# Staging the next sample's normalised input: low parts and transfers on POOL in four rows, two of them in the sum buffer

## The chip, the cores and the metric

One core of a Trainium2 chip. The metric is the device time of one execution in microseconds; the median of three runs counts. Engines are named as in the profile: PE is TensorE, ACT ScalarE, DVE VectorE, POOL GpSimd, and SP issues most transfers.

## The reference

The input is x with 8 samples of 512 channels and 32 x 32 positions (N = 1024). Two layers follow each other.

```python
# layer 0: attention without softmax, then batch norm over samples and positions
K, Q, V = conv1x1(X, Wq, bq), conv1x1(X, Wk, bk), conv1x1(X, Wv, bv)     # 8 heads of 64
M = einsum('bhmn,bhen->bhme', K, V)
Out = conv1x1(einsum('bhme,bhmn->bhen', M, Q), Wo, bo) + X
y = batch_norm(Out) * gamma + beta
# layer 1: group norm, 8-head softmax attention over 1024 positions, projection, residual
xn = group_norm(y, 32 groups) * gamma + beta
q, k, v = split(w_qkv @ xn + b_qkv)
a = softmax(q.T k / sqrt(64)) v
out = y + w_proj @ a + b_proj
```

## The kernel before

All large products are made from split operands. A float32 matrix is held as a high part (what ACT writes as fp32r) and a low part (the matrix less its high part), and a product is three matmuls: high x high, high x low and low x high.

Layer 0 runs over the 8 samples and ends at about 680 us of the span. It stores its result, not yet normalised, to DRAM (`y_dram`); its statistics give a scale and a bias per channel and sample for layer 1's group norm (`xn_scale`, `xn_bias`). The change touches layer 1 alone.

Layer 1 goes sample by sample, b = 0 to 7, and each sample in four pairs of heads (`PAIRS`). A pair has four tiles for the queries and keys, 16 tiles that only find the row maxima, and for each of 8 blocks of keys scores, exponentials (ACT, L685, into `probs`, a ring of three slots of 2 heads x 1024), weighing (PE, L1336, into `psum[2]`) and the running sum of the probabilities (POOL, L506, into `p_sum`). The tiles of the next pair are made among the scores of this one. A sample ends with 8 value tiles for the next sample (`v_tile`), among them the matmuls that add `p_sum` over the keys (`sums`, L1350), then 8 projection tiles, whose results are added to the residual on DVE (L1089). The residual is loaded into slots 0 and 1 of `probs` (`res32`), scaled by ACT (L713) and stored from there. Then come the next sample's pair 0 and its query and key tiles for pair 1 (L1285).

The normalised input of a sample must lie in SBUF as high and low parts (`xn`, 2 x 4 x 1024 per partition). There is room for one sample only, so that of sample b + 2 is *staged* while sample b ends: it is made from `y_dram` and stored to `xn_dram`, and SP loads it in one 4 MB transfer in the third pair of sample b + 1. Samples 1 to 7 are staged: sample 1 in the opening of layer 1, beside sample 0's value tiles and maxima, the other six at the ends of samples 0 to 5. The ends of samples 6 and 7 stage nothing.

Staging is done in 8 units of 512 columns (`UNITS`). For each, ACT waits for the unit's load into `y_half` (two halves in turn), normalises it in place (`norm_unit`, L602), writes its high part into slot 2 of `probs` (`stage_r`, L608), and DVE subtracts (`norm_lo`, L927) to write the low part beside it. ACT's queue then issues the store of both parts (`store_xn`, L593, 512 KB) and the load of the unit after the next (L596, 256 KB). SP loads the first two units of a sample (L388). Four units are made before ACT's `hid_hi` of the last pair, four after the residual is scaled. DVE's four early subtractions stand behind the copies of the first four value tiles (L966), the four late ones behind its adds of projection tiles 2 to 5.

Each engine works its own instructions in the order written, and semaphores order the engines among each other. `work_full` and `work_free` count PE's tiles and their evictions: tiles go through two banks, so PE starts tile n only when tile n - 2 is evicted. The six staging samples are one loop on SP, ACT and DVE (L435, L718, L1093); PE's loop holds samples 0 to 6 (L1447), POOL's too (L509).

ACT waits for all staging stores before the exponentials of a sample use slot 2 again.

Of the kernel before, what the change touches and what calls it, by code (L numbers as in the profile page):

```python
# [69 lines left out]
def build(nc, x, wq_t, wv_t, wk, wo_t, bq0, bv0, bk0, bo0, gamma0, beta0, gamma1, beta1, w1, bqkv1, bproj1, out):  # L70
# [14 lines left out]
    with ExitStack() as ctx:  # L85
# [42 lines left out]
        stage_r = probs[:, SLOTS - 1].rearrange("p h (a n) -> p h a n", a=2).bitcast(F32R)  # L128
        y_half = a1.take(2, HALF)
# [3 lines left out]
        recip = a1.take(NH, HALF)  # L133

# [75 lines left out]
        y_half_loaded = [sem("y_half_loaded0"), sem("y_half_loaded1")]  # L210
# [5 lines left out]
        xn_lo_done = sem("xn_lo_done")  # L216
        xn_stored = [sem("xn_stored0"), sem("xn_stored1")]
# [54 lines left out]
        UNITS = NH * CT  # L272
        EARLY = UNITS // 2

        def unit(u):
            return u // NH, slice(u % NH * HALF, (u % NH + 1) * HALF)
# [54 lines left out]
        def _(sp):  # L331
# [68 lines left out]
            load_y(1)  # L400
# [3 lines left out]
            def batch1(b, last, stage):  # L404
# [9 lines left out]
                if not last:  # L414

                    for half in xn_stored:
                        sp.wait_ge(half, (b + 1) * (UNITS // 2) * 16)
# [25 lines left out]
        def _(pool):  # L443
# [48 lines left out]


            def batch1(b, last):
                for p in range(PAIRS):
                    last_pair = last and p == PAIRS - 1
                    pairs = b * PAIRS + p
                    for i in range(1, NT):
                        for half in range(1 if last_pair else NH):
                            cols = slice(half * HALF, (half + 1) * HALF)  # L500
                            if i == 1 and half == 0:
# [5 lines left out]
                                               probs[:, i % SLOTS, :, cols], ALU.add).then_inc(sum_step, 1)  # L507

            with pool.Fori(0, B - 1) as b:  # L509
                batch1(b, False)  # L510
            batch1(B - 1, True)

        @block.scalar
        def _(act):
# [74 lines left out]
            def store_xn(tb, u):  # L589

                j, cols = unit(u)
                act.wait_ge(xn_lo_done, tb * UNITS + u + 1)
                act.dma_start(f(xn_dram[tb, :, :, j, cols]), f(stage_r[:, u % 2])).then_inc(xn_stored[u % 2], 16)  # L593
                if u + 2 < UNITS:
                    j, cols = unit(u + 2)
                    act.dma_start(y_half[:, u % 2], y_v[tb, :, j, cols]).then_inc(y_half_loaded[u % 2], 16)  # L596

            def norm_unit(tb, u, scale, bias):

                made = (tb - 1) * (UNITS // 2) + u // 2  # L600
                act.wait_ge(y_half_loaded[u % 2], (made + 1) * 16)
                act.activation(y_half[:, u % 2], y_half[:, u % 2], ACT.Identity, scale=scale(u // NH),  # L602
                               bias=bias(u // NH)).then_inc(xn_made, 1)
                act.wait_ge(xn_made, tb * UNITS + u + 1)
                if u >= 2:

                    act.wait_ge(xn_stored[u % 2], made * 16)
                act.activation(stage_r[:, u % 2, HI], y_half[:, u % 2], ACT.Copy).then_inc(xn_hi_done, 1)  # L608
                if u:
                    store_xn(tb, u - 1)  # L610
                if u == UNITS - 1:
                    store_xn(tb, u)
# [21 lines left out]
            for u in range(UNITS):  # L634
                norm_first(u)
            for i in range(QK):
                qk_hi(0, 0, i)
            for i in range(NT):
                act.wait_ge(v_first_full, i + 1)
                act.activation(v_t[:, i], bank(i % CT), ACT.Copy).then_inc(v_first_done, 1)  # L640
                norm_unit(1, i, lambda j: xn_scale[:, j, 1:2], lambda j: xn_bias[:, j, 1:2])

            def batch1(b, last, stage):
                work.start(b)
                for p in range(PAIRS):
# [10 lines left out]
                    for i in range(NT):  # L656
                        before = slot_row(i)
                        for half in range(NH):
                            cols = slice(half * HALF, (half + 1) * HALF)
                            act.wait_ge(scores_full, pairs * 2 * NT + 2 * i + half + 1)  # L660
                            if i < SLOTS and p == 0:
# [7 lines left out]
                                if i == SLOTS - 1 and half == 0:  # L669

                                    for stored in xn_stored:
                                        act.wait_ge(stored, (b if last else b + 1) * (UNITS // 2) * 16)
# [26 lines left out]
                def stage_units(us_):  # L699
                    for u in us_:  # L700
                        norm_unit(b + 2, u, lambda j: next_norm[:, 0, j:j + 1], lambda j: next_norm[:, 1, j:j + 1])

                if stage:
# [3 lines left out]
                    stage_units(range(EARLY))  # L707
# [7 lines left out]
                if stage:  # L715
                    stage_units(range(EARLY, UNITS))

# [6 lines left out]
        def _(dve):  # L724
# [200 lines left out]
            def norm_lo(tb, u):  # L925
                dve.wait_ge(xn_hi_done, tb * UNITS + u + 1)
                dve.tensor_tensor(stage_r[:, u % 2, LO], y_half[:, u % 2], f(stage_r[:, u % 2, HI]), ALU.subtract).then_inc(xn_lo_done, 1)  # L927

# [91 lines left out]
            for m in range(MAXES):  # L1020
                max_tile(m)
                if m % 2:
                    norm_lo(1, m // 2)
            max_join()

            def batch1(b, last, stage):
                work.start(b)
                for p in range(PAIRS):
# [20 lines left out]
                    if more:  # L1049
                        if p == 0:  # L1050
                            dve.wait_ge(max_ready, pairs + 1)
                        for m in range(MAXES):
# [3 lines left out]
                            if p == 1 and m == 4 and stage:  # L1056

                                dve.wait_ge(xn_hi_done, (b + 2) * UNITS)
# [25 lines left out]
                for t, (o, half) in enumerate(proj_tiles(last)):  # L1084
# [400 lines left out]
```

## Time and profile before

| | |
|---|---|
| median of 3 runs | 2802.01 us (2800.88 to 2802.41) |
| the profiled execution | 2800.88 us, span 2799.2 us |
| PE busy | 2644.6 us, 94% of the span |
| DVE / ACT / POOL busy | 1577.1 / 992.0 / 1122.4 us |
| mean granted clock of TensorE | 0.975 |
| `xn_dram` stores on ACT's queue | 56 of 512 KB, 3.4 us to landing |

The span runs from the first to the last instruction of the profiled execution. Busy time is the time in which an engine worked; what decides is when PE stands still, and what released it.

### The profile page before, as it was taken

What the parts mean: (1) busy time and instruction counts of PE and PEld (TensorE: products, weight loads), DVE (VectorE), ACT (ScalarE), POOL (GpSimd) and SP (SyncE); (2) the same over time, 40 slices, a digit from 0 to 9 for tenths busy, and PEclk for the clock granted to TensorE, in tenths of its full rate; (3) what the DMA queues carried; (4) which work ended last, traced back from release to release, by engine and by line L of the source; (5) the groups of instructions that cost most, each with busy time, mean ns of one, the idle gap of its engine ahead of it and who ended that gap; (6) DMA issues with size and microseconds to landing.
All of it is one profiled execution on the core that took longest, in us unless ns stands there. A gap on an engine that the chain in (4) does not pass through costs nothing.

```text
span 2799.2 us, 38416 instructions
## 1 busy us (share of the span) xinstructions
PE 2644.6 (94%) x13908; PEld 1740.0 (62%) x13908; DVE 1577.1 (56%) x1755; ACT 992.0 (35%) x1214; POOL 1122.4 (40%) x522
## 2 busy tenths in 40 slices
PE   8999999998899989998998999899989998999998
PEld 6888788886555565565556555655565565557554
DVE  5545455545566636754764566466636754764665
ACT  3232222332343433433442444343433433442433
POOL 3320000000076426534571576076426534671762
PEclk9999999998999999999999999999999999999999
DMA  5331111112301230232204110401230232202001
GB/s 184 127 118 35 40 45 60 60 60 91 120 24 76 80 125 23 91 104 86 83 31 161 51 76 34 171 23 76 79 125 23 91 105 85 91 16 105 16 16 61
DMA packets 75530, 214.53 MB, mean 77 GB/s; under 512 B 9712, under 2 KB 9712, under 8 KB 74480
## 3 DMA queue, kind: packets, MB, share of 16 engines
q1 hardware_dynamic: 50512, 159.41, 15.6%
q10 hardware_dynamic: 21280, 40.38, 4.3%
q0 software_dynamic: 3584, 12.58, 1.3%
q8 instruction: 109, 1.79, 0.3%
q14 instruction: 45, 0.37, 0.0%
HBM read 141.05 MB, written 71.30 MB: 76 GB/s over the span
## 4 chain that ended last, share of the span: by engine, by line
PE 76%; DVE 9%; DMA 5%; issue 3%; ACT 3%; POOL 3%; ACTq 1%; DVEq 0%; POOLq 0%
PE psum L1336 14%; PE psum L1285 13%; PE psum L1320 12%; PE psum L1103 12%; PE psum L1122 6%; PE psum L1295 6%; DMA a_all<-y_dram 5%; DVE small L944 4%; PE psum L1146 4%; PE psum L1174 3%; POOL a_all L506 2%; PE psum L1350 2%; PE psum L1217 2%; DVE a_all L974 1%; PE psum L1114 1%
## 5 line engine op out<-in xcount | busy, mean ns | idle before, releaser
L506 POOL TENSOR_TENSOR a_all<-a_all 128x1024 f32<-128x1024 f32 x441 | 1055.3, 2393 | 1027.2 <-ACT a_all L685 993.2
L944 DVE TENSOR_REDUCE small<-psum 128x2 f32<-128x1024 f32 x512 | 627.6, 1226 | 413.9 <-PE psum L1295 413.9
L685 ACT ACTIVATE a_all<-psum 128x1024 f32<-128x1024 f32 x512 | 500.4, 1023 | 561.2 <-PE psum L1320 529.5
L1320 PE MATMUL psum<-r_all 64*128 64x512 f32 x4096 | 528.3, 394 | 3.9 <-ACT a_all L685 1.7
L1336 PE MATMUL psum<-a_all 128*64 128x512 f32 x2048 | 497.3, 607 | 2.8 <-DVE a_all L974 2.8
L1103 PE MATMUL psum<-r_all 128*128 128x512 f32 x1920 | 473.2, 408 | 26.0 <-DVE a_all L966 20.2
L1103 PEld LDWEIGHTS psum<-r_all 128*128 128x128 f32 x1920 | 376.9, 198 | 125.2 <-DVE a_all L966 22.7
L1320 PEld LDWEIGHTS psum<-r_all 64*128 64x128 f32 x4096 | 378.4, 185 | 111.7 <-ACT a_all L685 25.8
L1285 PE MATMUL psum<-r_all 128*128 128x512 f32 x1536 | 386.1, 409 | 49.3 <-DVE a_all L1089 30.6
L1285 PEld LDWEIGHTS psum<-r_all 128*128 128x128 f32 x1536 | 297.2, 197 | 154.6 <-DVE r_all L935 33.8
L1295 PE MATMUL psum<-r_all 64*128 64x512 f32 x1024 | 235.8, 456 | 42.9 <-DVE small L944 42.4
L1336 PEld LDWEIGHTS psum<-a_all 128*64 128x64 f32 x2048 | 124.5, 136 | 232.2 <-issue 179.6
L1295 PEld LDWEIGHTS psum<-r_all 64*128 64x128 f32 x1024 | 95.8, 183 | 270.7 <-DVE small L944 261.7
L974 DVE RECIPROCAL a_all<-psum 128x512 f32<-128x512 f32 x64 | 214.4, 3351 | 13.1 <-PE psum L1350 13.1
L619 ACT ACTIVATE r_all<-psum,small 128x512 fp32r<-128x512 f32 x128 | 88.2, 689 | 325.3 <-PE psum L1285 325.0
L935 DVE SCALAR_TENSOR_TENSOR r_all<-psum,small,r_all 128x512 fp32r<-128x512 f32 x128 | 91.8, 717 | 196.4 <-ACT r_all L619 196.4
L491 POOL MEMSET r_all<- 128x128 f32 x1 | 0.2, 198 | 487.0 <-PE psum L1103 487.0
L1122 PE MATMUL psum<-r_all 128*128 128x512 f32 x768 | 178.5, 391 | 0.2 <-DVE small L844 0.2
L1122 PEld LDWEIGHTS psum<-r_all 128*128 128x128 f32 x768 | 143.4, 188 | 31.7 <-DVE small L844 1.0
L1146 PE MATMUL psum<-r_all 128*128 128x256 f32 (+2 forms) x768 | 135.4, 330 | 1.4 <-DVE r_all L734 1.4
L516 ACT ACTIVATE r_all<-psum 128x512 fp32r<-128x512 f32 (+2 forms) x128 | 68.8, 565 | 173.5 <-PE psum L1103 92.7
L1146 PEld LDWEIGHTS psum<-r_all 128*128 128x128 f32 x768 | 119.0, 189 | 10.4 <-DVE r_all L734 1.8
(116 smaller groups left out, 1696.5 us busy)
## 6 DMA issues: line engine op xcount, KB each, us to landing
r_all<-w_dram SPq DMA_DIRECT2D x48, 1024.0 KB, 4.9
xn_dram<-a_all ACTq DMA_DIRECT2D x56, 512.0 KB, 3.4
r_all<-xn_dram SPq DMA_DIRECT2D x7, 4096.0 KB, 13.8
a_all<-y_dram SPq DMA_DIRECT2D x9, 2048.0 KB, 9.2
a_all<-x SPq DMA_DIRECT2D x16, 1024.0 KB, 6.2
y_dram<-a_all SPq DMA_DIRECT2D x16, 1024.0 KB, 4.2
out<-a_all SPq DMA_DIRECT2D x32, 512.0 KB, 4.0
a_all<-y_dram ACTq DMA_DIRECT2D x42, 256.0 KB, 3.9
```

The source lines that it names most:

```text
L506: pool.tensor_tensor(p_sum[:, :, cols], probs[:, 0, :, cols] if i == 1 else p_sum[:, :, cols], probs[:, i % SLOTS, :, cols], ALU.add).then ...
L685: act.activation(probs[:, i % SLOTS, :, cols], psum[half][:, :, :], ACT.Exp, scale=SCALE).then_inc(probs_ready, 1)
L935: dve.scalar_tensor_tensor(out=to[:, par, LO, cols], in0=ps, scalar=bqkv_c[:, of_k * CT + pair:of_k * CT + pair + 1], in1=f(to[:, par, HI, ...
L944: dve.reduce_max(max2[:, :, tile, half], psum[3][:, :, :], AX_X).then_inc(work_free, 2)
L974: dve.reciprocal(recip[:, h], psum[2][:, h]).then_inc(sums_read, 1)
L1103: last = pe.matmul(to, w, m, start=(i == 0), stop=(i == len(pairs) - 1))
L1122: last = pe.matmul(to(o), stationary(w, j, o), moving(m, j), start=(j == 0 and i == 0), stop=(j == CT - 1 and i == 2))
L1146: last = pe.matmul(bank(g)[:, G0[g]:], xt[:, n % XT_SLOTS, w, g * P:(g + 1) * P], xt[:, n % XT_SLOTS, m, G0[g]:], start=(n == 0 and i == 0 ...
L1285: last = pe.matmul(to, w_s[:, slot, piece, w, j], xn[:, m, j, cols], start=(j == 0 and k == 0), stop=(j == CT - 1 and k == 2))
L1295: last = pe.matmul(psum[3][:, h], q_hl[rows_, par, HI, tile * P:(tile + 1) * P], k_hl[rows_, par, HI, half * HALF:(half + 1) * HALF], star ...
L1320: last = pe.matmul(psum[half][:, h], k[rows_], q[rows_], start=(t == 0), stop=(t == 3))
L1336: last = pe.matmul(psum[2][h * D:(h + 1) * D, half], v_t[:, i, head], probs[:, i % SLOTS, h, half * HALF:(half + 1) * HALF], start=(i == 0 ...
```

## The change

- The unit of staging is a row j of 1024 columns (one of the four 128-channel tiles). The high parts of rows j and j + 2 share `hi_slot[:, j % 2]`; both lie where `stage_r` lay, in slot 2 of `probs`.
- A row's data lies in `raw[j]`: rows 0 and 3 in `y_row` (in `y_half`'s place), rows 1 and 2 in the two halves of `p_sum`. The low part is written over it.
- ACT normalises and writes the high part (`norm_row`), and issues no transfer. One row is made before `hid_hi` of the last pair, three after the residual is scaled. In the opening a row follows every second value tile.
- POOL subtracts and issues the stores, high and low apart (512 KB each), the load of rows 1 and 2 (once the row sums of the sample's last pair are made) and, once row 0 is stored, that of row 3. SP loads row 0.
- DVE's `norm_lo` is gone.
- POOL waits for the staging stores before a sample's first add into `p_sum`, and its loop now ends with sample 5.

```diff
-        stage_r = probs[:, SLOTS - 1].rearrange("p h (a n) -> p h a n", a=2).bitcast(F32R)
-        y_half = a1.take(2, HALF)
+        hi_slot = probs[:, SLOTS - 1].bitcast(F32R)
+        y_row = a1.take(N)
...
+        raw = (y_row, p_sum[:, 0], p_sum[:, 1], y_row)
...
+        STORED = CT // 2 * 2 * 16
...
-            def load_y(tb):
-
-                sp.wait_ge(xn_lo_done, tb * UNITS)
-                for u in range(2):
-                    j, cols = unit(u)
-                    sp.dma_start(y_half[:, u], y_v[tb, :, j, cols]).then_inc(y_half_loaded[u], 16)
+            def load_y(tb, first=False):
+
+                if not first:
+                    sp.wait_ge(xn_stored[1], (tb - 1) * STORED)
+                sp.dma_start(y_row, y_v[tb, :, 0]).then_inc(y_loaded[0], 16)
...
+            def split_rows(tb):
+
+                pool.dma_start(p_sum, y_v[tb, :, 1:3]).then_inc(y_loaded[1], 16)
+                for j in range(CT):
+                    pool.wait_ge(xn_hi_done, FIRST_MADE + (tb - 1) * CT + j + 1)
+                    pool.tensor_tensor(raw[j].bitcast(F32R), raw[j], f(hi_slot[:, j % 2]), ALU.subtract).then_inc(xn_split, 1)
+                    pool.wait_ge(xn_split, (tb - 1) * CT + j + 1)
+                    pool.dma_start(f(xn_dram[tb, :, HI, j]), f(hi_slot[:, j % 2])).then_inc(xn_stored[j % 2], 16)
+                    pool.dma_start(f(xn_dram[tb, :, LO, j]), raw[j]).then_inc(xn_stored[j % 2], 16)
+                    if j == 0:
+
+                        pool.wait_ge(xn_stored[0], (tb - 1) * STORED + STORED // 2)
+                        pool.dma_start(y_row, y_v[tb, :, 3]).then_inc(y_loaded[2], 16)
+
+            pool.wait_ge(norm_ready, 1)
+            split_rows(1)
...
+            def batch1(b, last, stage):
+                for half in xn_stored:
+
+                    pool.wait_ge(half, (b if last else b + 1) * STORED)
...
+                if stage:
+
+                    pool.wait_ge(sums_full, ONE + (b + 1) * PAIRS)
+                    split_rows(b + 2)
...
+            def norm_row(tb, j, scale, bias):
+
+                made = FIRST_MADE + (tb - 1) * CT + j + 1
+                act.wait_ge(y_loaded[(0, 1, 1, 2)[j]], tb * 16)
+                act.activation(raw[j], raw[j], ACT.Identity, scale=scale, bias=bias).then_inc(xn_made, 1)
+                act.wait_ge(xn_made, made)
+                if j >= 2:
+
+                    act.wait_ge(xn_stored[j % 2], (tb - 1) * STORED + STORED // 2)
+                act.activation(hi_slot[:, j % 2], raw[j], ACT.Copy).then_inc(xn_hi_done, 1)
...
-                norm_unit(1, i, lambda j: xn_scale[:, j, 1:2], lambda j: xn_bias[:, j, 1:2])
+                if i % 2:
+                    norm_row(1, i // 2, xn_scale[:, i // 2, 1:2], xn_bias[:, i // 2, 1:2])
...
-                    stage_units(range(EARLY))
+                    norm_rows(range(1))
...
-                    stage_units(range(EARLY, UNITS))
+                    norm_rows(range(1, CT))
...
-                if m % 2:
-                    norm_lo(1, m // 2)
...
-                        if stage and i < EARLY:
-                            norm_lo(b + 2, i)
...
-                    if stage and 2 <= t < 2 + UNITS - EARLY:
-                        norm_lo(b + 2, EARLY + t - 2)
```

## Rows read from the trace of the kernel before

**Rows 1.** The page: busy time and share of each engine; the chain by engine.

```profile
PE 2644.6 (94%) x13908; PEld 1740.0 (62%) x13908; DVE 1577.1 (56%) x1755; ACT 992.0 (35%) x1214; POOL 1122.4 (40%) x522
PE 76%; DVE 9%; DMA 5%; issue 3%; ACT 3%; POOL 3%; ACTq 1%; DVEq 0%; POOLq 0%
```

**Rows 2.** Timeline of PE, end of sample 1: start, length, instructions, idle before, releaser.

```profile
1221.25 8.49 PE L1103 MATMUL psum<-r_all 128*128 128x512 f32 x36
1233.12 32.98 PE L1103 MATMUL psum<-r_all 128*128 128x512 f32 x132 [3.38 <-DVE a_all L966]
1271.07 5.49 PE L1285 MATMUL psum<-r_all 128*128 128x512 f32 x12 [4.96 <-DVE a_all L1089]
```

**Rows 3.** Windows: length, busy of PE, PEld, DVE, ACT, POOL (x), clock, DMA share, GB/s.

```profile
952.12:1024.06 71.94, 61.79 (x253) 48.21 (x251) 28.10 (x34) 21.60 (x27) 2.32 (x1) 0.93 0.49 169
1213.72:1286.60 72.88, 63.15 (x253) 49.06 (x251) 28.12 (x34) 21.59 (x27) 2.32 (x1) 0.91 0.49 167
1476.25:1552.10 75.85, 64.17 (x253) 49.99 (x251) 28.19 (x34) 21.59 (x27) 2.32 (x1) 0.89 0.47 160
...
2264.65:2335.27 70.62, 61.20 (x253) 47.83 (x251) 28.10 (x34) 20.31 (x26) 2.32 (x1) 0.93 0.50 172
2523.46:2582.16 58.70, 57.24 (x253) 45.51 (x251) 23.29 (x26) 9.08 (x10) 2.30 (x1) 1.00 0.30 108
```

**Rows 4.** Timeline of PE, end of sample 6, which stages nothing.

```profile
2531.00 38.42 PE L1103 MATMUL psum<-r_all 128*128 128x512 f32 x168
2569.25 2.88 PE L1285 MATMUL psum<-r_all 128*128 128x512 f32 x12
```

**Rows 5.** Timelines of ACT and DVE, end of sample 1.

```profile
1227.05 0.81 ACT L602 ACTIVATE a_all<-a_all,small 128x512 f32<-128x512 f32 x1 [9.46 <-DMA a_all<-y_dram]
...
1228.56 0.69 DVE L927 TENSOR_TENSOR a_all<-a_all 128x512 fp32r<-128x512 f32 x1 [3.21 <-ACT a_all L608]
...
1269.72 0.69 DVE L927 TENSOR_TENSOR a_all<-a_all 128x512 fp32r<-128x512 f32 x1 [8.33 <-ACT a_all L608]
```

**Rows 6.** Timeline of PE in the opening of layer 1.

```profile
709.34 0.50 PE L1295 MATMUL psum<-r_all 64*128 64x512 f32 x2 [0.30 <-DVE r_all L935]
...
721.50 0.50 PE L1295 MATMUL psum<-r_all 64*128 64x512 f32 x2
...
745.75 0.50 PE L1295 MATMUL psum<-r_all 64*128 64x512 f32 x2 [1.23 <-DVE small L944]
747.64 4.53 PE L1285 MATMUL psum<-r_all 128*128 128x512 f32 x12 [1.39 <-DVE small L944]
```

**Rows 7.** Branches of PE's loops (ns min/median/max, first and last start); ACT after its own.

```profile
L1447 PEldq COMPARE_BRANCH  x7: 83/5490/7049, 999.5 to 2565.3; - x7
L1447 PEldq COMPARE_BRANCH  x1: 5837/5837/5837, 1262.0 to 1262.0; - x1
L1261 PEldq COMPARE_BRANCH  x6: 76/210/259, 177.2 to 593.6; - x6
1275.03 1.28 ACT L619 ACT_TABLE_LOAD   x1 [5.34 <-issue]
```

**Rows 8.** Timelines of POOL and ACT; landing times of POOL's and ACT's 512 KB stores.

```profile
43.62 1.29 POOL L482 TENSOR_TENSOR r_all<-a_all,r_all 128x512 fp32r<-128x512 f32 x1
45.56 0.59 POOL L484 DMA_DIRECT2D w_dram<-r_all  x1 [0.65 <-POOL r_all L482]
...
1194.03 22.01 POOL L506 TENSOR_TENSOR a_all<-a_all 128x1024 f32<-128x1024 f32 x9
...
1213.83 1.03 ACT L697 ACTIVATE a_all<-psum 128x1024 f32<-128x1024 f32 x1 [3.23 <-PE psum L1336]
...
2541.49 4.63 ACT L713 ACTIVATE a_all<-a_all,small 128x1024 f32<-128x1024 f32 x4
...
DMA to landing us min/median/max: 3.0/3.0/7.7
DMA to landing us min/median/max: 3.1/3.4/9.1
```

More of the change, by code:

```diff
@@ L209, in build @@
         y_first_loaded = sem("y_first_loaded")
-        y_half_loaded = [sem("y_half_loaded0"), sem("y_half_loaded1")]
+        y_loaded = [sem("y_loaded0"), sem("y_loaded12"), sem("y_loaded3")]
         v_first_full, v_first_done = sem("v_first_full"), sem("v_first_done")
@@ L216, in build @@
         xn_lo_done = sem("xn_lo_done")
+        xn_split = sem("xn_split")
         xn_stored = [sem("xn_stored0"), sem("xn_stored1")]
@@ L269, in proj_used @@
             return b * WORK + (WORK0 + before + t)
[L272 to L276, printed above, removed]
+        FIRST_MADE = NH * CT
+        STORED = CT // 2 * 2 * 16
         MID = 5
@@ L399, in _ @@
                 sp.sem_inc(half, ONE)
-            load_y(1)
+            load_y(1, True)
             sp.wait_ge(work_full, QK)
@@ L416, in batch1 @@
                     for half in xn_stored:
-                        sp.wait_ge(half, (b + 1) * (UNITS // 2) * 16)
+                        sp.wait_ge(half, (b + 1) * STORED)
                     sp.dma_start(f(xn), f(xn_dram[b + 1])).then_inc(xn_loaded, 16)
@@ L507, in batch1 @@
                                                probs[:, i % SLOTS, :, cols], ALU.add).then_inc(sum_step, 1)
-            with pool.Fori(0, B - 1) as b:
-                batch1(b, False)
-            batch1(B - 1, True)
+                if stage:
+                    pool.wait_ge(sums_full, ONE + (b + 1) * PAIRS)
+                    split_rows(b + 2)
+            with pool.Fori(0, B - 2) as b:
+                batch1(b, False, True)
+            batch1(B - 2, False, False)
+            batch1(B - 1, True, False)
         @block.scalar
@@ L587, in norm_first @@
                 act.activation(xn[:, HI, j, cols], y_first[:, j, cols], ACT.Copy).then_inc(xn_hi_done, 1)
[L589 to L612, printed above, removed]
+            def norm_row(tb, j, scale, bias):
[6 more added lines that the diff above has]
+                act.activation(hi_slot[:, j % 2], raw[j], ACT.Copy).then_inc(xn_hi_done, 1)
             def qk_hi(pair, par, i):
@@ L633, in _ @@
             act.wait_ge(norm_ready, 1)
-            for u in range(UNITS):
+            for u in range(FIRST_MADE):
                 norm_first(u)
@@ L671, in batch1 @@
                                     for stored in xn_stored:
-                                        act.wait_ge(stored, (b if last else b + 1) * (UNITS // 2) * 16)
+                                        act.wait_ge(stored, (b if last else b + 1) * STORED)
                             elif i < SLOTS:
@@ L697, in batch1, with norm_rows @@
                     act.activation(o32, psum[2][:, :, :].rearrange("p a n -> p (a n)"), ACT.Copy).then_inc(o_ready, 1)
-                def stage_units(us_):
-                    for u in us_:
-                        norm_unit(b + 2, u, lambda j: next_norm[:, 0, j:j + 1], lambda j: next_norm[:, 1, j:j + 1])
+                def norm_rows(js):
+                    for j in js:
+                        norm_row(b + 2, j, next_norm[:, 0, j:j + 1], next_norm[:, 1, j:j + 1])
                 if stage:
@@ L1056, in batch1 @@
                             if p == 1 and m == 4 and stage:
[L1058 removed]
+                                dve.wait_ge(xn_hi_done, FIRST_MADE + (b + 1) * CT)
                                 for i, of in enumerate((xn_scale, xn_bias)):
```

4 lines of the change are left out of this document (removed).

## The prediction, made before the kernel was run

> **What bounds the kernel now.** I read the page's busy shares and its chain by engine first [rows 1]: TensorE is busy for 94% of the 2799.2 us span and 76% of the chain is its matmuls. So an edit of POOL, ScalarE or VectorE counts only where TensorE stands still or runs at its lower clock. Next I read TensorE in order of time where one sample of layer 1 ends and the next begins [rows 2]; I call this stretch the boundary. It holds the eight value tiles, the row sums, the eight projection tiles and the next pair's four query and key tiles. At the boundary shown TensorE stops for 3.38 us, released by VectorE's copy of a value tile (L966), and for 4.96 us, released by VectorE's last adds (L1089). The windows over all boundaries give the size; of six that stage a sample four are shown, with the one that doesn't (2523.46) [rows 3]. All seven hold the same 253 matmuls. The six last 71.94, 72.88, 75.85, 70.86, 72.72 and 70.62 us, the seventh 58.70. The excess is 13.24 + 14.18 + 17.15 + 12.16 + 14.02 + 11.92 = 82.7 us. Part of it is idle time (72.88 - 63.15 = 9.7 us, against 58.70 - 57.24 = 1.5 without staging), part is clock: granted 0.89 to 0.93, against 1.00, so stretches of it ran at 1.2 GHz and not 2.4. In the seventh the value and projection tiles run in one piece [rows 4].
>
> Who holds VectorE is read from VectorE's and ScalarE's own time [rows 5]: the subtraction L927 waited 3.21 and 8.33 us for ScalarE's L608, and ScalarE's L602 before it had waited 9.46 us for a 256 KB load. VectorE works in order, so a subtraction that waits for a transfer has an eviction standing behind it, and TensorE behind that.
>
> **What goes.** Eight subtractions of 0.69 us [rows 5] leave VectorE per staged sample, with every wait of VectorE on staging but one (before next_norm, L1058, 100 us after the rows are made). With nothing else late, each of the six boundaries becomes the seventh: -82.7 us. ScalarE loses its 14 DMA issues and gets four pairs of activations on 1024 columns in place of eight on 512.
>
> In the opening (sample 1 is staged beside the first value tiles and maxima) TensorE's first max tile starts at 709.34 and the sixteenth at 745.75 [rows 6]. The first six steps take 2.03 us each (721.50 - 709.34 over six), so fifteen would end at 739.74: 6.0 us are lost to VectorE, late behind L927. The next twelve matmuls take 4.53 us, against 2.88 at full clock [rows 4], so 1.65 more. Together -7.7 us.
>
> **What is late next.** With VectorE on time, TensorE's own loop branch comes into view. L1447's branch stands 5.49 us in the median and 7.05 at most, L1261's in layer 0 0.21 [rows 7]. The six taken branches of L1447 last 5.49, 5.84, 6.72, 7.05, 4.95 and 5.35 us (one row each, the second is shown), mean 5.90; the one not taken 0.08. The branch at 1262.0 starts 4.1 us before the queued matmuls end at 1266.10 (1233.12 + 32.98), and in the seventh boundary 3.96 us pass from the branch (2565.3) to the next tile, at 2569.25 [rows 4]. Two register instructions of 0.1 us follow it. So each loop return leaves a gap of 5.90 + 0.15 - 3.96 = 2.1 us, which today lies inside the 4.96. Six of them give back +12.6 us. Bounds: 0, if the branch only waits with TensorE, and 3.2 each (19 in all), if every one is like the 7.05.
>
> The trace alone can't tell a branch that fetches from one that stands with a stalled engine. The Trainium skill (Runtime: NRT & Kernel Launch, "Instruction fetch mechanics") says that a taken branch to a target outside the two pages held forces a fetch by DMA before execution goes on. By the rule the 12.6 us stay; by the other reading they fall away, and the sum is 12.6 us lower. The trace leans to the rule: the same branch not taken costs 0.08 us, and ScalarE, which waits for nothing there, stands 5.34 us before its table load [rows 7], of which two issues of stores are some 1.9. ScalarE's own return stays hidden (below).
>
> A gap can also take the clock down. Gaps of 3.38 and 4.96 us did; one of 1.46 didn't (clock 1.00 in the seventh boundary [rows 3]). A gap of 2.1 us lies between, nearer to the small one, with the spread of 5.90 on both sides. I take a drop in three of six, at the 1.65 us it costs twelve matmuls: +5 us; bounds 0 and 16 (six at 2.6, which is 5.49 - 2.88 [rows 2, 4]).
>
> **Does the new chain stay hidden?** Times are those of the boundary at 1213.72. ScalarE makes row 0 behind the copy L697, which ends at 1214.86 [rows 8] (its slot's last sums are long done): two activations at 1.16 (L713's four take 4.63; both forms at that price), to 1217.2. That ends before VectorE has the first half normalised, so hid_hi isn't late. POOL ends its adds at 1216.04 and then waits for the row sums (TensorE ends them at 1221.3 [rows 2]), because p_sum is what they read. It issues the 1 MB load (0.6 us), subtracts row 0 (2.4 us: L506 has 22.01 / 9 = 2.45 for 1024 columns, L482 1.29 for 512) and issues two stores of 0.6 us, with 0.65 before them: 1226.2. A store of 512 KB lands after 3.0 to 7.7 us from POOL's queue and 3.1 to 9.1 from ScalarE's [rows 8]; I take 5, since the 2 MB residual load is under way. Row 3's load is issued by 1231.8 and landed by 1237. VectorE, without its waits, follows the seventh boundary, where L713 starts 18.03 us after the first value tile: 1231.75 to 1236.4. Row 1 follows to 1238.7, row 2 to 1241.0. Row 3 needs its data (1237) and high slot 1 free: row 1's subtraction ends at 1241.1, its stores are issued by 1243.0 and landed by 1248.0. So ScalarE is done at 1249.2, and with its loop return (at most 5.34) and table load (1.28) at 1255.8. It is needed when TensorE ends the first query tile. In the seventh boundary that tile starts 45.79 us after the first value tile and lasts 2.88 [rows 4]; with the branch's 2.1 it ends at 1264.5. Slack 8.7 us. The last store lands at about 1257; its readers, POOL's first add and the third exponential, come more than 15 us later. With 9.1 us for each transfer ScalarE's end moves by 4.1 and the slack is 4.6. So: 0. Nor is anything gained there: ScalarE isn't what TensorE waits for.
>
> In the opening, POOL's chain starts after norm_ready; row 3 is done on ScalarE by 743, with the table load (1.28) by 744.0, and the first query tile ends at 744.5. Cover 0.5 us: cost 0, and up to 3 if it slips.
>
> POOL's subtraction beside VectorE: the Trainium skill (SBUF — State Buffer, "Who interferes with whom") says that a VectorE instruction with two SBUF inputs and a GpSimd one that reads SBUF shut each other out for the whole instruction. The VectorE instructions here with two SBUF inputs are the normalising products L982 and hid_lo L999, close before and after L713's start at 1231.75. By the rule they cost one subtraction each time that one meets them; by these times row 0's is done by 1225 and row 1's starts at 1238.7, so the rule takes nothing unless the chain slips by 5 us.
>
> **The sum.** The profiled execution's own time is 2800.88 (span 2799.20 and 1.68 around it). 2800.88 - 82.7 - 7.7 + 12.6 + 5 = 2728.1. It is the lowest of the three runs; their median is 1.1 higher, so I forecast 2729.
>
> **Rivals.**
> A. The branch gap isn't there (it stood with the engine), so all boundaries become the seventh: 2802.0 - 90.4 = 2712. For it: only TensorE shows such a long branch, VectorE's, equally in a long loop, takes 0.06 us. Against: ScalarE's 5.34.
> B. One of the two stops stays, with another releaser. The residual load now shares the DMA engines with a 1 MB load and 1 MB of stores and holds L713; or row 0's subtraction slides onto L982 and shuts VectorE out for 2.4 us where a value tile's eviction has hardly any room. The value-tile stop costs 3.38 and about 2 of clock, so 32 us over six: 2729 + 32 = 2761; with only the 2.4 it is 2743. Against: L713 is needed at about 1240, 3 us after it ends, and 24 us pass from the load's issue.
> C. Slower than before. POOL's software queue is slow and its transfers stand in a row: store 0, load 3, and store 1 before row 3's high part. ScalarE is then late for the first query tile and TensorE waits. With landing time T for each, it is done at the later of 1244.2 + T and 1229.2 + 2T, and late from 1264.5 - 6.6 = 1257.9 on, T = 13.7. Above T = 15 each us costs 2 us a boundary, and the net gain (13.8 - 2.9, and the opening's 1.3) is eaten at T = 20.4 (1.3 + 2 x 5.4 = 12.2). At T = 22 the kernel takes 2802 + 6 x 3.1 = 2821. For it: each transfer shares the engines with 2 MB and more. Against: nothing of 512 KB took longer than 9.1 us.
> D. The change does what it says and nothing moves, because TensorE's stops come from something else: 2802. Against: the seventh boundary, which differs in the staging alone.
>
> **How the numbers follow.** Forecast 0.60 (its own range 2719 to 2739, by the gap's bounds and the clock's), A 0.13, B 0.19, C 0.04, D 0.04. The range 2708 to 2759 takes in A and most of B. A measurement of this kernel can tell 0.2% (5.6 us) from no change. Faster: forecast, A, B and a little = 0.93; same 0.03; slower 0.04.
>
> **What would show it.** Windows of the same 253 matmuls at each staged boundary: 61 to 63 us, the unstaged one 58.7 as before. No stop in the value tiles; one of about 2 us after the projection tiles, whose end falls with the end of L1447's branch. Max tiles 2.03 us apart throughout the opening. POOL's four subtractions of 2.4 us, L713 beginning before 1233 on the old scale, and ScalarE waiting for TensorE, not for a DMA, at the first query tile. Wrong if TensorE stands in the value tiles, if the clock at the boundaries stays near 0.91, or if the third exponential of a sample waits for a store.

## The result and the profile after

The changed kernel takes 2731.09 us in the median (2729.09 to 2733.05, 4 runs) against 2801.45 for the kernel before beside it: a ratio of 0.9754, 95% interval 0.9739 to 0.9769. The forecast was 2729.

The page: TensorE's busy share rises, and its busy time falls by 24.6 us with the same 13908 matmuls, which fits work that no longer runs at the lower clock (granted clock at the boundaries 0.97 to 1.00, before 0.89 to 0.93) [rows 1, 3].

```profile
PE 2620.0 (96%) x13908; PEld 1724.6 (63%) x13908; DVE 1543.2 (57%) x1699; ACT 974.8 (36%) x1158; POOL 1228.6 (45%) x620
```

Windows over the same 253 matmuls at four of the seven boundaries, columns as in [rows 3]:

```profile
947.19:1009.89 62.70, 59.16 (x253) 46.65 (x251) 23.28 (x26) 19.13 (x19) 17.67 (x15) 0.97 0.55 194
1199.27:1261.77 62.50, 59.10 (x253) 46.58 (x251) 23.28 (x26) 19.14 (x19) 17.68 (x15) 0.97 0.54 194
...
1702.96:1763.84 60.88, 57.55 (x253) 45.45 (x251) 23.28 (x26) 19.13 (x19) 17.66 (x15) 1.00 0.56 199
...
2454.99:2513.67 58.68, 57.23 (x253) 45.51 (x251) 23.28 (x26) 9.08 (x10) 3.04 (x2) 1.00 0.30 108
```

The six staged boundaries now last 62.7, 62.5, 62.2, 60.9, 62.5 and 60.8 us, together 371.6; before they took 434.9. The unstaged one is as it was. TensorE's timeline at the end of sample 1, as in [rows 2, 4], has the fourteen tiles behind the row sums in one piece, and one stop, which no other engine released:

```profile
1206.80 38.42 PE L1103 MATMUL psum<-r_all 128*128 128x512 f32 x168
1247.16 4.59 PE L1285 MATMUL psum<-r_all 128*128 128x512 f32 x12 [1.94 <-issue]
...
1253.31 8.46 PE L1285 MATMUL psum<-r_all 128*128 128x512 f32 x36 [1.45 <-DVE r_all L941]
```

The branch of TensorE's loop, as in [rows 7] (ns: shortest, median, longest; then the first and last start in us):

```profile
L1447 PEldq COMPARE_BRANCH  x7: 83/5729/5935, 989.0 to 2496.8; - x7
```

At the end of sample 1 the branch starts at 1241.10 and lasts 5.80 us, to 1246.90; the next tile starts at 1247.16. The other two timelines show the chain that took VectorE's place. ScalarE at the same boundary (L723 scales the residual, L616 and L621 make a row):

```profile
1217.29 4.63 ACT L723 ACTIVATE a_all<-a_all,small 128x1024 f32<-128x1024 f32 x4
...
1231.78 1.06 ACT L621 ACTIVATE a_all<-a_all 128x1024 fp32r<-128x1024 f32 x1 [4.20 <-DMA xn_dram<-a_all]
1232.86 1.28 ACT L628 ACT_TABLE_LOAD   x1
1251.79 0.69 ACT L628 ACTIVATE r_all<-psum,small 128x512 fp32r<-128x512 f32 x1 [17.64 <-PE psum L1285]
```

POOL's (L496 subtracts, L498 is a store, L503 the load of row 3):

```profile
1208.39 2.40 POOL L496 TENSOR_TENSOR a_all<-a_all 128x1024 fp32r<-128x1024 f32 x1
1211.45 0.57 POOL L498 DMA_DIRECT2D xn_dram<-a_all  x1 [0.66 <-POOL a_all L496]
...
1216.48 0.53 POOL L503 DMA_DIRECT2D a_all<-y_dram  x1 [3.90 <-DMA xn_dram<-a_all]
1224.23 2.41 POOL L496 TENSOR_TENSOR a_all<-a_all 128x1024 fp32r<-128x1024 f32 x1 [7.22 <-ACT a_all L621]
...
1232.93 2.39 POOL L496 TENSOR_TENSOR a_all<-a_all 128x1024 fp32r<-128x1024 f32 x1 [0.28 <-ACT a_all L621]
```

Row 3's high part still waits 4.20 us for a store, but nobody waits for it: ScalarE is ready at 1234.1 and then stands 17.64 us for TensorE. In the opening the first max tile and the first query tile stand 32.3 us apart, against 38.3 in [rows 6]:

```profile
712.36 0.50 PE L1295 MATMUL psum<-r_all 64*128 64x512 f32 x2 [0.30 <-DVE r_all L941]
...
742.72 0.50 PE L1295 MATMUL psum<-r_all 64*128 64x512 f32 x2
744.61 3.02 PE L1285 MATMUL psum<-r_all 128*128 128x512 f32 x12 [1.39 <-DVE small L950]
```

### The profile page after: what moved, and what is told of

It is laid out like the page before. It is cut to its first block, busy times and chain, and to the rows that moved or that the text cites. A ratio compares the mean times of both kernels' runs of the same rounds, so it can differ in the third digit from the quotient of the medians.

```text
span 2729.7 us, 38115 instructions
## 1 busy us (share of the span) xinstructions
PE 2620.0 (96%) x13908; PEld 1724.6 (63%) x13908; DVE 1543.2 (57%) x1699; ACT 974.8 (36%) x1158; POOL 1228.6 (45%) x620
## 4 chain that ended last, share of the span: by engine, by line
PE 81%; DVE 8%; POOL 6%; issue 3%; ACT 2%; DVEq 0%; ACTq 0%; POOLq 0%
PE psum L1103 17%; PE psum L1336 13%; PE psum L1285 13%; PE psum L1320 11%; PE psum L1122 6%; PE psum L1295 5%; POOL a_all L524 5%; DVE small L950 4%; PE psum L1146 4%; PE psum L1174 3%; PE psum L1350 2%; PE psum L1217 2%; ACT a_all L695 1%; PE psum L1114 1%; PE psum L1372 1%
## 5 line engine op out<-in xcount | busy, mean ns | idle before, releaser
L524 POOL TENSOR_TENSOR a_all<-a_all 128x1024 f32<-128x1024 f32 x441 | 1055.7, 2394 | 674.5 <-ACT a_all L695 636.7
L1103 PE MATMUL psum<-r_all 128*128 128x512 f32 x1920 | 460.3, 401 | 5.8 <-DVE r_all L1005 5.8
L1103 PEld LDWEIGHTS psum<-r_all 128*128 128x128 f32 x1920 | 369.1, 194 | 99.4 <-issue 7.0
L1285 PE MATMUL psum<-r_all 128*128 128x512 f32 x1536 | 375.3, 401 | 30.0 <-DVE r_all L941 11.5
L1285 PEld LDWEIGHTS psum<-r_all 128*128 128x128 f32 x1536 | 289.0, 191 | 132.8 <-DVE r_all L941 33.3
L1295 PE MATMUL psum<-r_all 64*128 64x512 f32 x1024 | 235.7, 456 | 36.3 <-DVE small L950 35.3
L1122 PE MATMUL psum<-r_all 128*128 128x512 f32 x768 | 178.6, 391 | 0.9 <-DVE small L854 0.8
L1122 PEld LDWEIGHTS psum<-r_all 128*128 128x128 f32 x768 | 143.4, 188 | 32.5 <-DVE small L854 1.7
L1146 PEld LDWEIGHTS psum<-r_all 128*128 128x128 f32 x768 | 118.5, 189 | 10.9 <-DVE r_all L744 2.5
```

The costliest lines, as they stand in the source:

```text
L524: pool.tensor_tensor(p_sum[:, :, cols], probs[:, 0, :, cols] if i == 1 else p_sum[:, :, cols], probs[:, i % SLOTS, :, cols], ALU.add).then ...
L1103: last = pe.matmul(to, w, m, start=(i == 0), stop=(i == len(pairs) - 1))
L1122: last = pe.matmul(to(o), stationary(w, j, o), moving(m, j), start=(j == 0 and i == 0), stop=(j == CT - 1 and i == 2))
L1146: last = pe.matmul(bank(g)[:, G0[g]:], xt[:, n % XT_SLOTS, w, g * P:(g + 1) * P], xt[:, n % XT_SLOTS, m, G0[g]:], start=(n == 0 and i == 0 ...
L1285: last = pe.matmul(to, w_s[:, slot, piece, w, j], xn[:, m, j, cols], start=(j == 0 and k == 0), stop=(j == CT - 1 and k == 2))
L1295: last = pe.matmul(psum[3][:, h], q_hl[rows_, par, HI, tile * P:(tile + 1) * P], k_hl[rows_, par, HI, half * HALF:(half + 1) * HALF], star ...
```

## The experiments

### One part alone: POOL subtracts, the units stay (e1)

```diff
@@ vector
-                        if stage and i < EARLY:
-                            norm_lo(b + 2, i)
...
@@ gpsimd, behind a staging sample's adds (and once ahead of the loop)
+                for u in range(UNITS):
+                    pool.wait_ge(xn_hi_done, tb * UNITS + u + 1)
+                    pool.tensor_tensor(stage_r[:, u % 2, LO], y_half[:, u % 2], f(stage_r[:, u % 2, HI]), ALU.subtract).then_inc(xn_lo_done, 1)
```

> The kernel before with one part of the change alone: the eight subtractions of a staged sample are POOL's, everything else (units of 512 columns, loads and stores on ScalarE's queue) stays. Theory (TensorE's stops came from VectorE standing in a subtraction that waits for a transfer): the value-tile stop of 3.4 us and the one behind the adds go; ScalarE's chain of small loads ends near 1260 on the old scale, just before the first query tile needs it at 1264, so 2735 to 2745 us. Rival (the small transfers set the end and the change needed its rows): ScalarE still ends near 1271, TensorE now waits for ScalarE at the query tiles, only the value-tile stop is gained: about 2775 us.

Measured: 2771.96 us (ratio 0.9884, 0.9861 to 0.9907): the rival's price, though not its mechanism. TensorE's timeline at the end of sample 1:

```profile
1217.39 38.41 PE L1104 MATMUL psum<-r_all 128*128 128x512 f32 x168
1256.49 3.01 PE L1286 MATMUL psum<-r_all 128*128 128x512 f32 x12 [0.68 <-issue]
...
1264.88 10.84 PE L1286 MATMUL psum<-r_all 128*128 128x512 f32 x36 [5.27 <-DVE r_all L942]
```

ScalarE's, from the last unit to the first query tile:

```profile
1254.70 0.81 ACT L613 ACTIVATE a_all<-a_all,small 128x512 f32<-128x512 f32 x1 [6.25 <-DMA a_all<-y_dram]
...
1262.06 1.28 ACT L630 ACT_TABLE_LOAD   x1 [5.88 <-issue]
1263.36 0.69 ACT L630 ACTIVATE r_all<-psum,small 128x512 fp32r<-128x512 f32 x1
```

The stop in the value tiles is gone, so VectorE's wait did cause it. The chain of small loads on ScalarE also ends earlier: its last high part is made 46.3 us after the first value tile, against 56.0 before [rows 5]. That is where the theory had it (1260 on the old scale). What the theory left out stands behind it: two issues of stores (2.1 us), ScalarE's loop return (3.6 us) and the table load (1.3 us). So ScalarE itself is late: the first query tile was finished at 1259.5 and is read at 1263.36. The sixth staged boundary, where ScalarE's loop does not return, has its chain's end at 46.1 us, and TensorE's stop before the second query tile is the usual 1.46 us. At three of the others the chain itself ends later, at 49.5 to 51.2 us, and TensorE's stops are 6.2 to 10.9 us. Moving the subtraction turned one wait into another and kept under half of the gain.

### The other part alone: rows and transfers as after, VectorE subtracts (e2)

```diff
@@ gpsimd, split_rows
-                    pool.wait_ge(xn_hi_done, FIRST_MADE + (tb - 1) * CT + j + 1)
-                    pool.tensor_tensor(raw[j].bitcast(F32R), raw[j], f(hi_slot[:, j % 2]), ALU.subtract).then_inc(xn_split, 1)
@@ vector, behind value tile 0 and projection tiles 0, 1, 4; in the opening behind max tiles 3, 7, 11, 15
+                dve.wait_ge(xn_hi_done, FIRST_MADE + (tb - 1) * CT + j + 1)
+                dve.tensor_tensor(raw[j].bitcast(F32R), raw[j], f(hi_slot[:, j % 2]), ALU.subtract).then_inc(xn_split, 1)
```

> The kernel after with the other part alone: four rows and all transfers on POOL, but the four subtractions back on VectorE, each placed where its high part is made by then (behind value tile 0 and projection tiles 0, 1 and 4). Theory (it is the waiting and not the work that cost): 2731 us, within 4; VectorE has four operations of some 1.25 us in gaps of 2 us, each boundary 61 to 63 us. Rival (VectorE's work itself, or its place in the order, was the price): each of the four delays an eviction by up to 1.25 us, 2745 to 2760 us.

Measured: 2723.21 us (2719.1 to 2728.87; ratio 0.9722, 0.9695 to 0.9749). At the boundaries the rival is out: VectorE does the work in its gaps and TensorE does not wait for it. VectorE's timeline, two adds of projection tiles (L1097) with a subtraction between:

```profile
1220.85 0.69 DVE L1097 TENSOR_TENSOR a_all<-psum,a_all 128x512 f32<-128x512 f32 x1 [2.03 <-PE psum L1111]
1221.46 1.22 DVE L935 TENSOR_TENSOR a_all<-a_all 128x1024 fp32r<-128x1024 f32 x1
1223.57 0.69 DVE L1097 TENSOR_TENSOR a_all<-psum,a_all 128x512 f32<-128x512 f32 x1 [0.89 <-PE psum L1111]
```

In the opening it is not out. There the max tiles follow each other every 2.0 us, and a subtraction in between holds VectorE's next maximum (L952) and with it TensorE:

```profile
714.05 1.23 DVE L935 TENSOR_TENSOR a_all<-a_all 128x1024 fp32r<-128x1024 f32 x1 [1.11 <-ACT a_all L619]
716.47 0.51 PE L1303 MATMUL psum<-r_all 64*128 64x512 f32 x2 [1.30 <-DVE small L952]
```

Three such stops make the opening 36.1 us long, from the first max tile to the first query tile, against 32.3 in the after: 3.8 us, which POOL's subtraction saves.

That e2 is 8 us faster than the after all the same was in neither theory. Its loop branches last 5.47, 4.60, 5.70, 5.01, 3.91 and 4.75 us, against 5.94, 5.80, 5.68, 5.73, 5.81 and 5.69; its boundaries sum to 360.2 us, 11.4 less. Whether that is all is asked in e11.

### TensorE's loop written out, in the after (e3) and in the before (e4)

```diff
-            with pe.Fori(0, B - 1) as b:
+            for b in range(B - 1):
                 batch1(b, False)
```

> The kernel after with TensorE's loop over the samples of layer 1 written out, so that no branch is taken there. Theory (the branch fetches, and it alone is left of the boundary's excess): the six stops of 1.8 to 2.1 us go (11.5 us) and with them the four stretches at the lower clock (6.7 us of the twelve matmuls behind): 2713 us, every boundary 58.7 us. Rival (the branch only waits with TensorE for something else, or straight code pays at its page crossings as much): 2731 us, the stops stay with another releaser.

> The kernel before with TensorE's loop over the samples of layer 1 written out. Theory (the fetch lay inside the wait for VectorE's last adds): no change, 2801 us within 3, the stop of 4.4 to 6.5 us stays as it is. Rival (the fetch lengthened the stop): up to 12 us faster, 2789.

Measured: e3 2713.33 us (2708.53 to 2713.85; ratio 0.9674, 0.9651 to 0.9698), e4 2800.96 (ratio 0.9997, 0.9984 to 1.001). All seven boundaries of e3 last 58.69 us. TensorE's timeline in e3, end of sample 1:

```profile
1201.66 38.42 PE L1103 MATMUL psum<-r_all 128*128 128x512 f32 x168
1239.91 2.88 PE L1285 MATMUL psum<-r_all 128*128 128x512 f32 x12
...
1244.36 8.46 PE L1285 MATMUL psum<-r_all 128*128 128x512 f32 x36 [1.46 <-DVE r_all L941]
```

and in e4:

```profile
1232.11 31.84 PE L1103 MATMUL psum<-r_all 128*128 128x512 f32 x132 [3.00 <-DVE a_all L966]
1268.89 4.94 PE L1285 MATMUL psum<-r_all 128*128 128x512 f32 x12 [4.94 <-DVE a_all L1089]
```

The same edit is worth 18 us behind the change and nothing ahead of it. So the branch's wait was there all along, inside the wait for VectorE's adds. Rival A is refuted by the stops of the after and by e3. e3 is faster than both kernels.

The traces also show what the branch waits for. The profile lists a DMA queue of kind `instruction` (packets, MB, share of the 16 engines). Below are the branch of the after from 1241.1 to 1246.9, then the whole span of the after, then that of e3:

```profile
q8 instruction: 1, 0.02, 1.0%
...
q8 instruction: 109, 1.79, 0.3%
...
q8 instruction: 93, 1.52, 0.2%
```

All 66 taken branches of L1447's loop, over the eleven profiled kernels that keep it, hold exactly one such packet of 16 KB. It starts 1.5 to 4.7 us after the branch, takes 0.9 to 1.2 us, and the branch ends 1.3 to 1.5 us behind it. In the same stretch of e3 there is none. The branch is a fetch of instructions, and what varies in it is the time before the packet starts.

### How much lateness POOL's chain has to spare (e5, e6)

```diff
+                    if j == 1 and not isinstance(tb, int):
+                        for k in range(IDLE):      # 9 in e5, 22 in e6
+                            pool.wait_ge(idled, (tb - 2) * IDLE + k + 1)
+                            pool.tensor_tensor(scratch, scratch, scratch, ALU.mult).then_inc(idled, 1)
                     pool.tensor_tensor(raw[j].bitcast(F32R), raw[j], f(hi_slot[:, j % 2]), ALU.subtract).then_inc(xn_split, 1)
```

> The kernel after with nine idle operations on POOL (512 columns, some 1.4 us each, about 12 us) before the subtraction of row 1, in the six boundaries alone. The after's trace has ScalarE done, table load included, at 1234.1 and needed at 1251.8: 17.6 us of slack. Theory (the chain through POOL is hidden by that slack): 2731 us within 4; ScalarE's copy of row 3 waits 12 us longer for the store and nothing else moves. Rival (the chain sets the boundary's end already): 2731 + 6 x 12 = 2803.

> The same with 22 idle operations, about 31 us before row 1's subtraction. Theory (slack 17.6 us, beyond it each us is paid at each boundary, as rival C of the prediction had it): 31 - 17.6 = 13.4 us late for the first query tile, six times, and some 2 us of clock each: 2731 + 80 + 10 = about 2821, that is slower than before. Rival (POOL's lateness is absorbed further by the two-tile buffering): below 2780.

Measured: e5 2727.66 us (2 runs, 2724.29 to 2731.04), e6 2786.35 (2785.43 to 2789.11; ratio 0.995, 0.9933 to 0.9967). POOL and ScalarE in e6 (L497 idles, L633 is row 3's high part, L640 the first query tile's):

```profile
1232.17 24.53 POOL L497 TENSOR_TENSOR scratch<-scratch 128x512 f32<-128x512 f32 x22 [7.26 <-ACT a_all L633]
```

```profile
1264.12 1.06 ACT L633 ACTIVATE a_all<-a_all 128x1024 fp32r<-128x1024 f32 x1 [28.69 <-DMA xn_dram<-a_all]
1265.20 1.28 ACT L640 ACT_TABLE_LOAD   x1
1266.49 0.69 ACT L640 ACTIVATE r_all<-psum,small 128x512 fp32r<-128x512 f32 x1
```

The theory holds: some 10 us cost nothing, 24.5 us cost 54.7 us over the six boundaries, which sum to 426.3. The size was wrong, for two reasons. An idle operation takes 1.11 us and not 1.4, so e6 idles 24.5 us. And the slack of 17.6 us held the branch's stop and the slow first tile, which are shorter in e6 (a stop of 0.84 us, a tile at full clock): the first query tile ends 49.8 us after the first value tile here, against 52.5. The slack is 14.9, the lateness 24.5 - 14.9 = 9.6 us, and TensorE's stop before the second query tile 10.98 with the usual 1.45 in it.

### What the branch's length hangs on (e7, e8)

```diff
@@ e7
-                    sp.dma_start(out_v[b, :, o], res32[:, o]).then_inc(out_stored[o // 2], 16)
+                    sp.dma_start(out_v[b, :, o, 0:64], res32[:, o, 0:64]).then_inc(out_stored[o // 2], 16)
@@ e8, behind the weight load that follows the store of o == 1
+                            sp.dma_start(spare, y_v[0]).then_inc(spared, 16)
```

e7 leaves the rest of the output out.

> The kernel after with the output stores cut to 64 of 1024 columns (the rest of the output is left out), so that less is in flight when TensorE takes its loop branch. Theory (the branch waits for a fetch that shares the DMA engines with the transfers in flight): the branch falls from 5.8 us to 3.5 to 4.5, the stop from 1.9 to 0 to 1, with less of the lower clock: 2715 to 2722 us. Rival (the branch's length is its own): 5.8 us and 2731.

> The kernel after with one more transfer, 2 MB from DRAM to DRAM that nobody reads, issued behind the weight load some 5 us before TensorE's loop branch. Theory (fetch beside transfers): the branch grows from 5.8 us to 7 or more, each stop by the same, the clock falls at all six boundaries: 2740 to 2755 us. Rival (its own length): 5.8 us and 2731.

Measured: e7 2719.64 us (ratio 0.9709, 0.9683 to 0.9736), e8 2735.25 (ratio 0.9765, 0.9739 to 0.9792). The branch in e7, then a window over one of them (its length, busy times of the engines, clock, DMA share, GB/s):

```profile
L1447 PEldq COMPARE_BRANCH  x7: 83/4990/5510, 988.3 to 2486.1; - x7
```

```profile
1238.30:1243.50 5.20, 4.15 (x19) 3.10 (x17) 1.38 (x2) 0.00 (x0) 0.00 (x0) 1.00 0.58 228
```

and in e8:

```profile
L1455 PEldq COMPARE_BRANCH  x7: 83/6077/6417, 987.4 to 2498.9; - x7
```

```profile
1239.50:1245.60 6.10, 4.13 (x19) 3.08 (x17) 1.38 (x2) 0.00 (x0) 0.00 (x0) 1.00 1.01 392
```

Both moved the way of the theory. e7's time is in its range, but its branches (4.9 to 5.5 us) are longer than the 3.5 to 4.5 expected. e8's grew by a quarter of the size expected; the DMA engines were at a share of 0.8 already in the after. e6 gives a third point nobody had planned: its late stores leave the engines at a share of 0.31, and the branch lasts 4.69 us in the median:

```profile
L1459 PEldq COMPARE_BRANCH  x7: 83/4687/4730, 988.7 to 2551.2; - x7
```

```profile
1248.90:1253.60 4.70, 4.17 (x19) 3.12 (x17) 1.18 (x2) 0.00 (x0) 4.34 (x5) 1.00 0.31 120
```

So 4.7, 5.0, 5.7 and 6.1 us go with shares of 0.3, 0.6, 0.8 and 1.0. The difference lies ahead of the instruction packet, which starts 2.3 to 2.4, 2.6 to 3.2, 3.3 to 3.6 and 3.5 to 4.0 us after the branch. The share isn't all: e2's shortest branch (3.91 us) fell into a stretch with a share of 0.99, and its packet started after 1.5 us. Which transfers lengthen it, and when, stays open.

### POOL beside VectorE's products (e9)

The nine idle operations of e5 stand before row 0's subtraction.

> The kernel after with the nine idle operations (two reads from SBUF, about 12 us) before the subtraction of row 0, so that POOL works beside VectorE's two normalising products, its copies of value tiles and hid_lo. The rule on the shared port says that the products and hid_lo, with two SBUF inputs, wait for a whole POOL operation when it came first: up to 1.4 us for each of four, 1 us or less of it seen by TensorE, whose next value tile has 0.3 us of room: 2731 to 2742 us, with a value-tile stop of up to 1 us and gaps before L988 and L1005. The other theory (no exclusion between these): 2731, VectorE's times as before. The chain's 12 us are inside the slack either way, by the after's trace.

Measured: 2731.86 us (2725.37 to 2742.64; ratio 0.9784, 0.976 to 0.9808). VectorE (L1000 normalises, L1017 is hid_lo), which takes 0.68 and 0.74 us for these in the after:

```profile
1208.12 0.96 DVE L1000 TENSOR_TENSOR a_all<-a_all 128x512 f32<-128x512 f32 x1
...
1212.16 0.94 DVE L1017 SCALAR_TENSOR_TENSOR r_all<-a_all,small,r_all 128x512 fp32r<-128x512 f32 x1
...
1214.88 1.05 DVE L1017 SCALAR_TENSOR_TENSOR r_all<-a_all,small,r_all 128x512 fp32r<-128x512 f32 x1
```

POOL at the same time:

```profile
1201.88 10.67 POOL L497 TENSOR_TENSOR scratch<-scratch 128x512 f32<-128x512 f32 x9
1212.51 2.87 POOL L508 TENSOR_TENSOR a_all<-a_all 128x1024 fp32r<-128x1024 f32 x1
```

The two do touch: the products and hid_lo take 0.2 to 0.3 us longer, row 0's subtraction 2.87 instead of 2.40. The rows say how. The last idle operation ends at 1212.55 and the hid_lo beside it 0.55 us later, at 1213.10; row 0's subtraction ends at 1215.38 and the next hid_lo at 1215.93, again 0.55 us later. So each waits for what is left of POOL's operation, and here only 0.4 to 0.5 us was left. Where more is left, more is paid. In the middle of a sample of the after, hid_lo (L1005) starts 1 us into one of POOL's adds (L524):

```profile
1065.18 2.37 POOL L524 TENSOR_TENSOR a_all<-a_all 128x1024 f32<-128x1024 f32 x1 [16.05 <-ACT a_all L695]
1066.21 1.89 DVE L1005 SCALAR_TENSOR_TENSOR r_all<-a_all,small,r_all 128x512 fp32r<-128x512 f32 x1
1067.63 2.71 POOL L524 TENSOR_TENSOR a_all<-a_all 128x1024 f32<-128x1024 f32 x1
```

It takes 1.89 us instead of 0.74 and ends 0.55 us behind the add's end at 1067.55; the next add takes 2.71 instead of 2.37. The Trainium skill (SBUF — State Buffer, "Who interferes with whom") has such a pair hold an exclusive lock, with the later one blocked until the first has finished; the trace agrees. In e9 it cost little because the idle operations are short, and TensorE's value tiles have no stop. A subtraction of 2.4 us that starts just ahead of one of VectorE's products was not tried.

### Why the after and e2 differ (e11), and ScalarE's own loop return (e10, e12)

e11 is e2 with TensorE's loop written out. e10 and e12 put 70 and 160 fulfilled waits at the end of ScalarE's loop body.

> The rows with VectorE's subtractions (as in e2_dve_rows) and TensorE's loop over the samples written out. Theory (e2 was 8 us faster than the after only because its loop branches happened to be shorter, 3.9 to 5.7 us against 5.7 to 5.9): without branches it equals e3_after_pe_unrolled, 2713 us within 4, every boundary 58.7. Rival (POOL's share in the subtraction costs something of its own, or VectorE's does): 2705 or 2721.

> The kernel after with 70 waits that are long fulfilled at the end of ScalarE's loop body, which then has 376 instructions, more than the 367 of before (the after has 306). Theory (a long enough body must be fetched again at the loop's return): 3.7 us between ScalarE's branch and the next instruction, as before, against 0.26; hidden, so 2731 us within 4. Rival (the 3.7 us came from ScalarE's own transfers or from where it stood): 0.26 stays.

> The kernel after with 160 fulfilled waits at the end of ScalarE's loop body; 70 gave 35 recorded instructions (341 in the body, still 0.27 us behind the branch), so 160 should give about 386, above the 367 of before. Theory (length of the body decides whether it must be fetched again): about 3.7 us behind ScalarE's branch, hidden, 2729 us. Rival (length doesn't matter): 0.27 us.

Measured: e11 2713.9 us (2710.68 to 2716.87; ratio 0.967, 0.9655 to 0.9686), all boundaries 58.69. At the boundaries it therefore makes no difference which engine subtracts, and what e2 gained there were its shorter branches. The opening is 36.3 us in e11 against 32.6 in e3, as in e2; these 3.7 us are lost in the spread of the whole times. For e2 the two make 11.4 - 3.8 = 7.6 us of the 8.

e10 2728.98 and e12 2727.97 us (2 runs each). In the trace, the time from ScalarE's loop branch to its next recorded instruction, by recorded instructions in the loop:

| kernel | instructions | us | packets of the second instruction queue (q14), whole span |
|---|---|---|---|
| after | 306 | 0.26 | 21 |
| e10 | 341 | 0.26 | 21 |
| before | 367 | 3.7 | 45 |
| e12 | 386 | 6.2 to 6.4 | 47 |

e10's body was shorter than its expectation said, since two waits make one record. The body of e12 begins where that of the after does, so it is the length that decides whether the return costs anything. e6 shows the same on POOL, where 237 instructions (e5) go with 0.24 us and 21 packets, and 263 with 3.5 to 3.8 us and 46 packets. The packets say that these returns are fetches too. e12's return costs more than the 3.7 us expected, which stays unexplained. Whether the place at which a body begins counts as well was not tried.

## Why the prediction was right

**The bound and the excess.** The unstaged boundary as a model of the staged ones held to 0.02 us: in e3 and e11 all seven are 58.69. The six lost 63.3 us, against 82.7 - 12.6 - 5 = 65.1 foretold.

**The branch.** Foretold 2.1 us a stop, measured 2.09, 1.94, 1.82, 1.88, 1.95 and 1.84, together 11.5 against 12.6. e3 shows it as a cause, and e4 that it lay inside the wait for VectorE before. It is a fetch: one instruction packet in every taken branch, none where the loop is written out. The Trainium skill's "Instruction fetch mechanics" (Runtime: NRT & Kernel Launch) has a taken branch to a target outside the pages held force a fetch by DMA before execution goes on; the trace agrees. The prediction said that the trace alone can't tell; the instruction queue in it could (the branch of before at 1262.0 holds one packet too).

**The clock.** Foretold three drops of six at 1.65 us, measured four: the twelve matmuls behind the stop took 4.4 to 4.6 us at four boundaries and 3.0 at two. The stops of 1.82 to 2.09 us at those four and of 1.88 and 1.84 at the other two don't differ in size. In e10 and e12, whose programs for TensorE are the same, it was three of six, and the largest stop that left the clock up was 2.15 us. So the count was a good guess; that the size of the gap decides, as the prediction argued, is not borne out at this size. In e4 even a stop of 3.39 us in the value tiles was followed by a granted clock of 1.00.

**The opening.** 6.05 us of pace and 1.5 of clock, against 6.0 and 1.65.

**Hidden or not.** Right in the sign, the slack mis-sized: 8.7 foretold, 17.6 in the trace. The term that failed is ScalarE's loop return, put at 5.34 us at most. It costs nothing there (0.26 us, while the last high part is still being made), because the body lost its transfers' instructions and fell from 367 to 306; I had treated it as a property of the loop's return, not of its length. The rest is the later end of the first query tile (1.7) and a chain that ended 1.9 us sooner, with stores landed in 3.9 us and not 5.

**The sum.** 63.3 + 7.6 = 70.9 us; the spans differ by 69.5. Another 3.0 us were lost ahead of the first max tile (712.36 against 709.34), before anything the change touches, and 1.6 us were gained in small pieces between the boundaries. Over the fourteen profiled kernels the first max tile moved between 705.1 and 712.4; its cause wasn't looked for. So the terms of the sum were right to 2 us. That the total came as close is in part luck, since this one point moves by 7 us from kernel to kernel.

**The rivals.** A is refuted by the after and e3. B's price never fell due in the after. The meeting it feared is real: in e9 it cost 0.2 to 0.3 us, because little was left of POOL's operations, and elsewhere in the traces it costs 1.15; its 2.4 was not tried. C had the right last step, as e6 shows with idle operations: a late ScalarE makes TensorE wait, from a point further off than foretold. Slow transfers, its cause, did not occur. D is refuted by the result, and by e1 and e2 in parts: e1 takes the stop in the value tiles away and hands the other to ScalarE, e2 takes both.

What the prediction didn't ask is which half of the change does it. The rows count at the boundaries; POOL's subtraction adds only the 3.8 us of the opening. Which part of the rows counts (their size, the earlier loads, the transfers taken off ScalarE) was not tested one by one.

## What to carry to other kernels

When an engine that evicts for TensorE waits for a transfer, look for the transfer chain first: shortening it (fewer and larger pieces, loaded ahead, issued by an idle engine) paid 78 us, moving the waiting operation alone to an idle engine 30. Before pricing a stall as gone, read which other wait ends inside it; a branch record of TensorE of several us with an instruction packet in it is such a one, and writing that loop out gave another 18 us. A loop's return on ScalarE or POOL is free up to some length of the body, so count instructions before adding to it.

## What the runs showed of the hardware

A taken branch on TensorE in a loop with 2827 recorded instructions lasts 3.9 to 7.1 us and holds one 16 KB instruction packet; in a loop with 890 it lasts at most 0.26 us. On ScalarE the return was free at 341 recorded instructions, cost 3.7 us at 367 and 6.2 at 386; on POOL it was free at 237 and cost 3.5 at 263. The queue q14 carried 21 packets in the first cases and 45 to 47 in the others. The median of TensorE's rose with the DMA share around it, with e2's 3.9 us as the exception. A VectorE operation with two SBUF inputs that starts beside a POOL operation with two ends 0.55 us after POOL's: 0.94 to 1.05 us instead of 0.74 in e9, 1.89 in the after. POOL's next one takes 2.87 instead of 2.40 and 2.71 instead of 2.37.
